# Context attention: GpSimd instead of VectorE splits the row maxima into bf16 parts, one step behind each of a unit's first four chunks

## What is computed

```python
attn = jnp.einsum('bhqd,bhkd->bhqk', q, k) * scale
attn = jnp.clip(attn, -CLAMP, CLAMP)          # layer 0 only
attn = jax.nn.softmax(attn, axis=-1)
x = jnp.einsum('bhqk,bhkd->bqhd', attn, v).reshape(B, Nq, Cq)
```

## Time and profile before

| what | us |
|---|---|
| median of 3 runs | 6515.49 |
| lowest and highest of them | 6505.90 and 6515.85 |
| the profiled execution | 6520.41 |
| its span, first to last instruction | 6518.0 |
| TensorE, VectorE, ScalarE, GpSimd busy | 5340.4, 4697.5, 3029.6, 2056.1 |

### The profile page before, as it was taken

How to read it: one execution, slowest core, us unless ns; L and a number is a source line. 1 busy time by engine, 2 the same in 40 slices (tenths; PEclk the granted TensorE clock), 3 DMA queues, 4 the chain that set the end, 5 groups by cost and what they waited for, 6 DMA issues and landing times. The chain is left out here.

```text
span 6518.0 us, 129937 instructions
## 1 busy us (share of the span) xinstructions
PE 5340.4 (82%) x45929; PEld 2778.1 (43%) x45975; DVE 4697.5 (72%) x8463; ACT 3029.6 (46%) x4548; POOL 2056.1 (32%) x2623
## 2 busy tenths in 40 slices
PE   3588856888888849968597999998766999999669
PEld 2243343222222234424356888886434333333234
DVE  6466966999999945457656777774565999999654
ACT  0233323777777722223433444444323777777522
POOL 0201535777777730004026555550025000000000
PEclk6799977999999969989796888887977999999879
DMA  2221045222222210002344333433137222222100
GB/s 67 45 47 22 9 138 185 59 62 58 58 62 59 52 53 1 0 9 103 118 142 119 113 113 116 117 114 103 52 91 230 60 65 67 65 65 67 56 12 13
DMA packets 740085, 486.52 MB, mean 75 GB/s; under 512 B 512088, under 2 KB 673472, under 8 KB 733952
## 3 DMA queue, kind: packets, MB, share of 16 engines
q1 hardware_dynamic: 739584, 479.45, 25.9%
HBM read 281.75 MB, written 196.37 MB: 73 GB/s over the span
## 5 line engine op out<-in xcount | busy, mean ns | idle before, releaser
L1507 ACT ACTIVATE c0a_raised<-c0a_sb 128x1024 f32<-128x1024 f32 (+1 forms) x832 | 836.3, 1025 | 318.2 <-PE c0a_sb L1318 313.9
L1271 POOL TENSOR_SCALAR c0a_prob<-c0a_raised 128x1024 f32<-128x1024 f32 (+1 forms) x832 | 864.7, 1039 | 365.1 <-ACT c0a_raised L1507 333.6
L1507 ACT ACTIVATE c1a_prob<-c1a_sb 128x1024 f32<-128x1024 f32 (+1 forms) x832 | 828.4, 1029 | 201.1 <-PE c1a_sb L1318 197.3
L1395 DVE TENSOR_REDUCE c1a_pmax<-c1a_sa 128x2 f32<-128x802 f32 (+1 forms) x704 | 697.9, 991 | 64.6 <-PE c1a_sa L1286 62.1
L1395 DVE TENSOR_REDUCE c0a_pmax<-c0a_sa 128x2 f32<-128x802 f32 (+1 forms) x704 | 696.8, 990 | 55.5 <-PE c0a_sa L1286 52.3
L1286 PE MATMUL c0a_sa<-c0a_K,c0a_Q 48*128 48x401 bf16 (+1 forms) x2048 | 471.5, 350 | 182.2 <-DVE c0a_pmax L1395 105.7
L1286 PE MATMUL c1a_sa<-c1a_K,c1a_Q 48*128 48x401 bf16 (+1 forms) x2048 | 465.0, 345 | 103.8 <-DVE c1a_pmax L1395 44.5
L1337 PE MATMUL c0a_pv<-c0a_prob,c0a_V 128*9 128x256 f32 x6656 | 525.9, 387 | 4.7 <-POOL c0a_prob L1271 4.1
L1337 PE MATMUL c1a_pv<-c1a_prob,c1a_V 128*9 128x256 f32 x6656 | 517.9, 382 | 0.9 <-issue 0.5
L1286 PEld LDWEIGHTS c0a_sa<-c0a_K,c0a_Q 48*128 48x128 bf16 x2048 | 128.8, 93 | 669.9 <-DVE c0a_pmax L1395 356.8
L3110 PE MATMUL dd_lb<-dd_src 64*128 64x128 f32 (+1 forms) x3584 | 356.2, 345 | 39.0 <-DVE dd_AB L3301 15.7
(11 more groups left out here) (609 smaller groups left out, 10726.6 us busy)
## 6 DMA issues: line engine op xcount, KB each, us to landing
dd_src<-unit_in SPq DMA_DIRECT2D x32, 1024.0 KB, 7.9
k_ctx<-c0k_parts SPq DMA_DIRECT2D x16, 1200.8 KB, 5.7
c0a_K<-k_ctx SPq DMA_DIRECT2D x128, 150.1 KB
k_ctx<-c1k_parts SPq DMA_DIRECT2D x16, 1200.8 KB, 6.0
c1a_K<-k_ctx SPq DMA_DIRECT2D x128, 150.1 KB
unit_in<-ds_raw SPq DMA_DIRECT2D x32, 512.0 KB, 2.6
unit_v<-ds_vs SPq DMA_DIRECT2D x32, 512.0 KB, 2.6
unit_in<-dp_res SPq DMA_DIRECT2D x32, 512.0 KB, 3.0
```

The lines of the kernel that those rows point to most:

```text
L1271: pool.tensor_scalar(prob[0:r, in_ring(v, c), :, :, :], raised[0:r, in_ring(v, c), :, :, :], 1.0, math.exp(-FLOOR), ALU.min, ALU.max).then ...
L1395: dve.tensor_reduce(pmax[:, u, :, 2 * pr + s, k], sa2[:, :, 0:w], AX.X, ALU.max).then_inc(a_reduced, 1)
L1507: act.activation(dst[0:r, in_ring(v, c), :, :, :], sb_[0:r, in_both(v, c), :, :, :], ACT.Exp).then_inc(b_exp, 1)
```

## The change

Of the steps of the maxima, `negm` and `held` stay with VectorE (`D_STEPS`, 2 steps with the clip and 1 without). The four operations of the split go to GpSimd, in the function `split`. For unit n+1 GpSimd issues step k right behind its clip of chunk k of unit n (k is 0 to 3); where there is no clip, they follow each other. Step k waits on `m_step` for the one before, thus step 0 for VectorE's last step, and step 0 also for the `m_turn` that read `mcols` last. VectorE's `negm` gets a wait for the end of the former unit's split.

```diff
+        D_STEPS = M_STEPS - 4
...
+                def split(n, k):
+
+                    pool.wait_ge(m_step, n * M_STEPS + D_STEPS + k)
+                    if k == 0:
+                        if n >= 1:
+                            pool.wait_ge(a_scored, base(n) + m_at(n - 1) + 1)
+                        ins = pool.tensor_copy(mcols[:, :, 0, :], held[:, :, :])
+                    elif k == 1:
+                        ins = pool.tensor_tensor(mrest[:, :, :], held[:, :, :], mcols[:, :, 0, :], ALU.subtract)
+                    elif k == 2:
+                        ins = pool.tensor_copy(mcols[:, :, 1, :], mrest[:, :, :])
+                    else:
+                        ins = pool.tensor_tensor(mcols[:, :, 2, :], mrest[:, :, :], mcols[:, :, 1, :], ALU.subtract)
+                    ins.then_inc(m_step, 1)
+
+                for k in range(4):
+                    split(0, k)
+                for n in range(UNITS):
+                    for c in range(KT):
+                        if clip:
+                            b_clip(n, n % 4, c)
+                        if c < 4 and n + 1 < UNITS:
+                            split(n + 1, c)
...
                     if step == 0:
                         dve.wait_ge(a_reduced, base(n + 1))
+                        if not early(n, 1):
+                            dve.wait_ge(m_step, n * M_STEPS)
...
                     else:
...
+                        dve.wait_ge(m_step, n * M_STEPS + 1)
+                        ins = dve.tensor_scalar(held[:, :, :], negm[:, :, :], -CLAMP, CLAMP - FLOOR, ALU.max, ALU.min)
                     ins.then_inc(m_step, 1)
...
-                for step in range(M_STEPS):
+                for step in range(D_STEPS):
                     m_part(0, 0, step)
...
-                            if step < M_STEPS and i < M_AT:
+                            if step < D_STEPS and i < M_AT:
```

More of the change, by code:

```diff
@@ L1412, in m_part @@
                     u = v % 2
-                    done = n * M_STEPS
                     if step == 0:
                         dve.wait_ge(a_reduced, base(n + 1))
+                        if not early(n, 1):
+                            dve.wait_ge(m_step, n * M_STEPS)
                         ins = dve.tensor_reduce(negm[:, :, :].rearrange("p e x -> p (e x)"),
```

## The result

The changed kernel takes 6449.42 us against 6510.69 us, medians of four runs each, 61 us less; the ratio is put at 0.9898 with a 95% interval of 0.9881 to 0.9914, which would be 66 us (the two medians alone give 0.9906). Timed a second time beside other kernels it took 6450.06 against 6524.9, 75 us less, ratio 0.9887 (0.9871 to 0.9904). The forecast was 93 us. The changed kernel came out alike both times; it is the kernel before that differs by 14 us between the two sets. The profiled execution took 6455.06 us, with a span of 6453.3.

What follows compares the result with a forecast made beforehand. VectorE, its split steps waiting for GpSimd's clips, was taken to bound `c0a`, with TensorE waiting for it. Gains of 79 (units), 12 (clock) and 2 (`c1a`) sum to 93 us: 6515.5 - 93 = 6422.5 us, range 6398 to 6468.

Steps and rivals of the forecast that it cites:

- The stretched steps: `c0a`: VectorE's four split steps, 2.56 us per unit, wait for GpSimd's clips; without them 1.64 us less per unit.
- `held` meets no clip: `c0a`: `held`, left on VectorE, falls between the clips of chunks 0 and 1, and takes about 0.17 us.
- The wait: `c0a`: in-order GpSimd waits for `held`, delaying the clips of chunks 1 and 2; unit 17.35 us instead of 18.62.
- T: `c0a`: the moment `held` is done on VectorE, 2.07 us after group 0 starts.
- p: Cost of one split step on GpSimd, taken as 0.20 us, with 0.15 and 0.45 as ends.
- 16.95 + 2p: `c0a` unit time in us by the path over chunk 2's clip; 17.35 as forecast.
- 16.32 + 4p: `c0a` unit time in us by the second path, over chunk 4's clip; takes over from p = 0.32.
- TensorE's waits for clips: `c0a`: `b_values` waits for clips twice per unit, 0.2 to 0.3 us each; waits in chunks 5 to 12 would be wrong.
- The clock: `c0a`: TensorE's nine falls to half clock, 1.3 us each, were expected to vanish, gaining 12 us.
- `c1a`: Stage without clips: VectorE loses four steps, 0.03 us in each of 62 units, gaining 2 us.
- the third rival: A split step costs GpSimd 0.3 to 0.45 us, unit 17.5 to 18.1, total 6437 to 6483 us; chance 0.15.
- GpSimd is never late: Rival: `held` comes earlier, chunk 1's clip is in time; unit 17.02, total 6402 us; chance 0.12.

Runs made afterwards that it cites:

- e4_memset: Kernel before the change, with GpSimd's clip of each chunk replaced by a memset of prob that reads nothing; 6422.24 us in its one run.
- e5_c1a_only: The change made in `c1a` alone, VectorE splitting as before in `c0a`; ratio 1.0004 to the kernel before.
- e1_chunk_later: The changed kernel with each split step issued one chunk later, behind the clips of chunks 1 to 4; 6412.27 us, ratio 0.9829 to the kernel before.
- e2_step_twice: The changed kernel with one further unused 128x8 tensor_tensor on GpSimd ahead of each split step; 6491.4 us, ratio 0.995.
- e3_dve_at_once: Kernel before the change, VectorE doing the four split steps in a row behind `held` (in `c1a` behind group 1); ratio 1.0208, 138 us slower.
- e6_two_later: The changed kernel with each split step issued two chunks later, behind the clips of chunks 2 to 5; 6510.55 us, ratio 0.9989.

## Why the prediction came out as it did

The direction, the place and the mechanism were right, and the time of 6449 lies in the range of 6398 to 6468, but the forecast of 93 us was a quarter to a half more than the medians show (75 and 61). Step by step:

- **The stretched steps.** Right: VectorE's four steps waited for clips, and on GpSimd they take 0.19 to 0.20 us. e4_memset shows the cause: with nothing changed but GpSimd's operation, two of the four are no longer stretched.
- **`held` meets no clip.** Right, 172 ns at most.
- **The wait.** Right in every station: forecast for the `b_values` of chunk 1 was T + 1.40, measured T + 1.44; for that of chunk 2 T + 2.72, measured 1705.40, T + 2.84; `m_turn` T + 5.19, measured T + 5.32.
- **The term that was mis-sized: p.** I put 0.20, the duration of the 128x8 operation, on top of the pitch of 1.12. The clips of chunks 1 to 4 start at 1702.90, 1704.31, 1705.68 and 1707.09, 1.40 apart in the mean, so a step costs 0.28 there. That number stood in the earlier trace rows as the distance from a start to a dependent start, 3455.73 to 3456.01; the duration was the wrong one of the two. With 0.28 the formula 16.95 + 2p gives 17.51 and 16.32 + 4p gives 17.44; measured is 17.47. That is 62 x 0.12 = 7 us of the forecast.
- **TensorE's waits for clips.** I expected two idle times of 0.2 to 0.3 us per unit. Its matmuls show one, of 0.29 us (16.7 us in 57 waits from 1200 to 2200 us). Its weight loads (PEld) waited for a clip about eight times per unit (460 times), some of them in chunks 5 to 12, which the prediction had named as a sign of being wrong. In the unit shown, the `b_values` of chunks 1 to 5 all start 0.05 to 0.08 us behind the end of their clips, so GpSimd catches up one or two chunks later than forecast. The unit time is still what the two paths give.
- **The clock.** Right that the falls go: after the first units there is none. Mis-sized: I priced one fall at 1.3 us from a single one, while in the profile of before seven falls in the 49 units of the steady part cost 918.5 - 49 x 18.62 = 6.1 us, 0.9 each, so nine are 8 us, not 12.
- **`c1a`.** 2 us expected, none found (e5_c1a_only), though so little is below what the runs tell apart.
- **Sum.** 71 + 8 = 79 us; measured between the first and the last `m_turn` are 76 and 78. The medians of the whole program show 61 and 75. The other stages scatter by some 5 us in single executions and the kernel before by 14 us between sets of runs; which of the two is nearer stays open.

The measured 6449 lies in the interval of the third rival, a step that costs 0.3 to 0.45 us (6437 to 6483), and p = 0.28 is just below it: the truth was between the forecast and this rival. Of the other rivals, that GpSimd is never late, 6402, was wrong for this kernel; but its unit of 17.02 is nearly that of e1_chunk_later, 16.90, at 6412 the fastest version here and 38 us below the change. The price at which the change would lose, p = 0.58, follows from the formula that e2_step_twice confirmed at 0.44.

## What to carry to other kernels

A tiny operation that lasts several times as long in one stage as in another is waiting for something, and its end gives it away: look at what ends at that instant on the other engines. When it is moved to an engine that works in order, price it by what is queued behind its wait, and put it behind the last item that must not be late; from the best place, one chunk earlier cost 35 us and one later about 100 (62 units of 0.57 and of 1.63 us), with the work itself unchanged. For a step between others take the distance of starts, not the duration.

## What the runs showed of the hardware

- VectorE waits for a GpSimd operation only in certain pairs: with a GpSimd operation that reads and writes SBUF all four steps were stretched, with one that only writes (memset, 0.95 us) the casts were (716 and 791 ns) and the `tensor_tensor`s were not (167 ns).
- A long idle time of TensorE can cost more than itself. One of 1.65 us per unit was followed by the half clock in each of four units in a row (e3_dve_at_once), one of 1.39 us in two of four (e6_two_later). In e2_step_twice the matmuls waited almost as long, (67.1 + 8.1) / 52.5 = 1.4 us per unit, but in pieces of 0.5 us at most, and the clock stayed at 1.00 over 950 us, as in the changed kernel. The kernel before, with 1.8 us per unit in pieces of up to 0.7, fell in about one unit of seven.
